# A state-space layer on one core: a new order of work inside a step on four engines

## The reference

```python
xn = layernorm(x)                                   # (2, 1024, 512)
proj = einsum('bld,pd->blp', xn, in_proj_w)         # gate 4096, x 4096, B 1024, C 1024, dt 64
xBC = silu(causal_conv(proj[x, B, C], taps=4) + conv_bias)
dt = softplus(dt + dt_bias); dA = exp(-dt * exp(A_log))
state = state * dA + (dt * x) (outer) B             # per head, 64 heads of 64, 128 states
y = state . C + x * D                               # scan over the tokens
yn = y * rsqrt(mean(y*y over a group of 512) + eps) * norm_weight * silu(gate)
s = einsum('bli,di->bld', yn, out_proj_w)
g = silu(xn @ W.T + bias + lora(xn))
out = x + s * g
```

## Time and profile before

| | |
|---|---|
| median of 3 runs | 1976.13 us (1975.52 to 1976.61) |
| the profiled execution | 1979.57 us, its span 1977.8 us |
| mean granted TensorE clock | 0.968 |
| busy: PE, DVE, POOL, ACT | 90%, 76%, 64%, 55% |
| steps 0 to 127: first and last output product | 137.5 us, 1970.2 us |

### The profile page before, as it was taken

How to read it: one execution, slowest core, us unless ns; L and a number is a source line. 1 busy time by engine, 2 the same in 40 slices (tenths; PEclk the granted TensorE clock), 3 DMA queues, 4 the chain that set the end, 5 groups by cost and what they waited for, 6 DMA issues and landing times.

```text
span 1977.8 us, 31470 instructions
## 1 busy us (share of the span) xinstructions
PE 1787.2 (90%) x10792; PEld 1373.7 (69%) x10792; DVE 1507.0 (76%) x1711; ACT 1087.7 (55%) x2843; POOL 1260.1 (64%) x1255
## 2 busy tenths in 40 slices
PE   7989989898998989899788998989899898989976
PEld 5767767676776767677566776767677676767754
DVE  8858778686877868687666877868687787868785
ACT  4566555655655565555445555565565556555543
POOL 6438475674847567484787847567484756748466
PEclk9999999999999999999899999999999999999988
DMA  7545445353544545355675554546354454635445
GB/s 254 156 139 171 142 136 170 120 181 105 167 145 138 169 121 181 108 172 162 181 232 156 170 147 139 168 122 181 106 169 144 136 165 125 181 107 155 146 135 162
DMA packets 322414, 304.75 MB, mean 154 GB/s; under 512 B 88272, under 2 KB 255568, under 8 KB 322256
## 3 DMA queue, kind: packets, MB, share of 16 engines
q1 hardware_dynamic: 321216, 302.60, 50.9%
q10 hardware_dynamic: 1040, 0.16, 0.0%
HBM read 246.57 MB, written 56.10 MB: 153 GB/s over the span
## 4 chain that ended last, share of the span: by engine, by line
POOL 42%; issue 31%; DVE 15%; ACT 9%; PE 2%; DMA 1%; SPq 0%; POOLq 0%; ACTq 0%; DVEq 0%
POOL cpre L1259 14%; POOL skip L1282 6%; POOL wconv_lo L1160 5%; POOL square L1305 4%; DVE ynt_lo L1140 4%; POOL wout_lo L1160 4%; POOL wgate_lo L1166 4%; ACT ps_y L807 4%; DVE xc L922 3%; DVE out_sum L1134 2%; POOL rstd_col L1313 2%; ACT stage L869 2%; DVE ps_y L1108 1%; POOL square_sum L1308 1%; POOL out_sum L1212 1%
## 5 line engine op out<-in xcount | busy, mean ns | idle before, releaser
L922 DVE SCALAR_TENSOR_TENSOR xc<-ps_conv,convw_sb,xc 128x511 f32<-128x511 f32 (+2 forms) x576 | 430.2, 747 | 149.9 <-ACT xc L693 136.4
L1305 POOL TENSOR_TENSOR square<-square 128x256 f32<-128x256 f32 x128 | 95.1, 743 | 442.9 <-ACT square L848 442.9
L1057 DVE TENSOR_TENSOR_SCAN decay<-decay,eye 128x1024 f32<-128x1024 f32 x125 | 362.9, 2903 | 0.0
L1259 POOL TENSOR_TENSOR cpre<-cpre,xc 128x1024 f32<-128x1024 f32 x112 | 300.4, 2682 | 0.0
L1350 PE MATMUL ps_out<-wout_hi,ynt_hi 128*128 128x512 f32 x512 | 161.6, 442 | 124.9 <-DVE out_sum L1134 105.6
L838 ACT ACTIVATE dtx<-x_tok,prefix_dt 128x64 f32<-128x64 f32 x1024 | 257.3, 336 | 6.5 <-DMA b_tok<-turned_d 6.5
L820 ACT ACTIVATE mean_square<-ps_g,eps 128x1 f32<-128x1 f32 x128 | 33.5, 261 | 409.9 <-PE ps_g L1343 409.9
L1509 PE MATMUL ps_y<-decay,dtx 128*64 128x128 f32 x1984 | 192.6, 281 | 32.5 <-DVE decay L1077 29.6
L1350 PE MATMUL ps_conv<-xn_hi,wconv_hi 128*128 128x512 f32 x768 | 217.7, 405 | 0.0
L1350 PEld LDWEIGHTS ps_out<-wout_hi,ynt_hi 128*128 128x128 f32 x512 | 98.4, 206 | 168.6 <-DVE out_sum L1134 129.3
L1134 DVE SCALAR_TENSOR_TENSOR out_sum<-ps_out,rstd_col,out_sum 128x512 f32<-128x512 f32 x108 | 80.5, 745 | 166.4 <-POOL rstd_col L1313 138.1
(11 more groups left out here) (233 smaller groups left out, 4105.6 us busy)
## 6 DMA issues: line engine op xcount, KB each, us to landing
decay<-decays_d SPq DMA_DIRECT2D x125, 512.0 KB, 5.0
cpre<-rows_d SPq DMA_DIRECT2D x112, 512.0 KB, 3.8
turned_d<-squares SPq DMA_DIRECT2D x512, 80.0 KB, 1.8
stage<-w_in_t SPq DMA_DIRECT2D x32, 1024.0 KB, 5.3
x_tok<-turned_d SPq DMA_DIRECT2D x128, 256.0 KB, 3.3
stage<-w_out_t SPq DMA_DIRECT2D x16, 1024.0 KB, 5.6
stage<-w_in_t SPq DMA_DIRECT2D x32, 256.0 KB, 3.2
b_tok<-turned_d SPq DMA_DIRECT2D x128, 64.0 KB, 3.6
```

The source lines that it names most:

```text
L922: e.scalar_tensor_tensor(acc[:, d:], ps[:, 0:BLK - d], convw_sb[:, tile, TAPS - 1 - d:TAPS - d], acc[:, d:], ALU.mult, ALU.add).then_inc(S ...
L1057: e.tensor_tensor_scan(d, d, eye8[:, :, :].rearrange("p h i -> p (h i)"), 0.0, ALU.mult, ALU.add).then_inc(scanned(i)[0], 1)
L1259: e.tensor_tensor(cpre[k % 2][:, :, :], cpre[k % 2][:, :, :], xc[i // CPB % 2][:, XT + 1, block_cols(i % NCH)].unsqueeze(1).to_broadcast([ ...
L1305: e.tensor_tensor(square[:, 0:2 * P], square[:, 0:2 * P], square[:, 2 * P:], ALU.add).then_inc(S["sum1"], 1)
```

## The change

In each step the instructions are the same; their order inside the step is another.

- **POOL** before: `skip`, splits of weights, `cpre`, both adds of squares, `rstd_col`, state decay, `xw`, edges. After: edges, `cpre`, `skip`, first add of squares, `rstd_col`, second add, state decay, `xw`, splits.
- **ACT** before: late convolution, `mean_square`, late SiLU, split of `wout`, `dtx`, `square`, early convolution, `ynt_hi`, gate SiLU, seed. After: late convolution, `dtx`, late SiLU, `square`, `mean_square`, `ynt_hi`, early convolution, seed, split of `wout`, gate SiLU. The halves of the gate's split and B and C's are at `at` = 3, 4 and 5 in place of 3, 5 and 4. From step 124 on the seed stays behind the gate SiLU.
- **DVE**: the scan is ahead of the late tile's taps, `last` stays behind them; the mixing matrix is ahead of the early tile's taps.
- **SP**: the tokens of the next step are fetched right after their store; the fetches of B and C's weights, of the x part's and of `wout` come one step later.

```diff
@@ sync
                 if i + 1 < N:
                     store_turned(i + 1)
+                    fetch_tokens(i + 1)
...
-                    if at == 3:
+                    if at == 4:
                         fetch_conv_bc(g + 1)
-                    if at == 5 and left > 1:
+                    if at == 6 and left > 1:
                         fetch_conv_x(g + 2)
-                    if at == 6:
+                    if at == 7:
                         fetch_out(g + 1)
-                if i + 1 < N:
-                    fetch_tokens(i + 1)
@@ scalar
                 if 0 <= m < N and conv_late(m) is not None:
                     conv(conv_late(m))
-                if u >= 0:
...
-                    e.activation(mean_square[:, u % 2:u % 2 + 1], ps_g[:, 2 * P:2 * P + 1], ACT.Identity, bias=eps[:, :],
-                                 scale=1.0 / GC).then_inc(S["var2"], 1)
-                if 0 <= m < N and conv_late(m) is not None:
-                    silu(conv_late(m))
-                if i < N and at == 1:
-                    w.wait_ge(S["scaled"], XT * (g + 1))
-                    w.wait_ge(S["mm_ffn"], KT + TOK)
-                    w.wait_ge(S["mm_out"], NCH * g)
-                    split_hi(wout_hi, staged(0, DM), range(XT), S["hi_out"])
                 if i < N:
...
                     scaled.then_inc(S["dtx"], 1)
+                if 0 <= m < N and conv_late(m) is not None:
+                    silu(conv_late(m))
                 if 0 <= m < N:
...
                     e.activation(square[:, :], y_bank(m)[:, :], ACT.Square).then_inc(S["square"], 1)
-                if i < N and conv_early(i) is not None:
-                    conv(conv_early(i))
+                if u >= 0:
+                    w.wait_ge(S["mm_ssq"], u + 1)
+                    w.wait_ge(S["rstd2"], u - 1)
+                    w.wait_ge(S["half"], 2)
+                    e.activation(mean_square[:, u % 2:u % 2 + 1], ps_g[:, 2 * P:2 * P + 1], ACT.Identity, bias=eps[:, :],
+                                 scale=1.0 / GC).then_inc(S["var2"], 1)
                 if 0 <= m < N:
...
                     e.activation(ynt_hi[:, :, :], turns(y_bank(m)), ACT.Copy).then_inc(S["hi2"], 1)
+                if i < N and conv_early(i) is not None:
+                    conv(conv_early(i))
+                if i < TAIL:
+                    seed(i)
+                if i < N and at == 1:
+                    w.wait_ge(S["scaled"], XT * (g + 1))
+                    w.wait_ge(S["mm_ffn"], KT + TOK)
+                    w.wait_ge(S["mm_out"], NCH * g)
+                    split_hi(wout_hi, staged(0, DM), range(XT), S["hi_out"])
                 for k in gated(i):
                     gate_silu(k)
+                if TAIL <= i < N:
+                    seed(i)
                 if i < N:
-                    seed(i)
                     if at == 3 and left:
                         split_gate(g + 1, (0, 1))
-                    if at == 5 and left:
+                    if at == 4 and left:
                         split_gate(g + 1, (2, 3))
...
-                    if at == 4 and left:
+                    if at == 5 and left:
                         split_conv_bc(g + 1, range(KT))
@@ vector
-                if 0 <= m < N and conv_late(m) is not None:
-                    taps(conv_late(m))
...
                     if i <= TAIL:
                         scan(i)
+                if 0 <= m < N and conv_late(m) is not None:
+                    taps(conv_late(m))
+                if i < N:
+                    if i <= TAIL:
+                        last_factors(i)
                     if i + 1 < N:
                         turn(i + 1)
...
+                if i <= TAIL:
+                    mixing_matrix(i)
                 if i < N and conv_early(i) is not None:
                     taps(conv_early(i))
-                if i <= TAIL:
-                    mixing_matrix(i)
@@ gpsimd
+                if i < N and i % NCH == 0:
+                    edges(group(i))
+                if i < N and i % NCH > 0:
+                    left_of_state(i)
                 if i < N:
...
                                     ALU.mult).then_inc(S["skip"], 1)
+                if 0 <= m < N:
+                    bm, cm, gm = batch(m), m % NCH, group(m) % GROUPS
+                    w.wait_ge(S["square"], m + 1)
+                    e.tensor_tensor(square[:, 0:2 * P], square[:, 0:2 * P], square[:, 2 * P:], ALU.add).then_inc(S["sum1"], 1)
+                if u >= 0:
+                    col = slice(u % 2, u % 2 + 1)
+                    w.wait_ge(S["var2"], u + 1)
+                    w.wait_ge(S["osum"], u - 1)
+                    e.tensor_tensor(rstd_col[:, col], mean_square[:, col], half[:, :], ALU.pow).then_inc(S["rstd2"], 1)
+                if 0 <= m < N:
+                    w.wait_ge(S["sum1"], m + 1)
+                    w.wait_ge(S["mm_ssq"], m)
+                    e.tensor_tensor(square_sum[:, :], square[:, 0:P], square[:, P:2 * P], ALU.add).then_inc(S["sum2"], 1)
+                    if cm < NCH - 2:
...
+                        e.tensor_tensor(by_head(dec[:, :]), by_head(new[:, :]), heads_bc(total_bc[:, first:first + GH]),
+                                        ALU.mult).then_inc(S["sdec"], 1)
+                if i < N and i % NCH < NCH - 1:
+                    scale_x(i)
                 if i < N:
                     g, at = divmod(i, NCH)
                     left = BATCH * GROUPS - 1 - g
...
-                if i < N and i % NCH > 0:
-                    left_of_state(i)
-                if 0 <= m < N:
...
-                if i < N and i % NCH < NCH - 1:
-                    scale_x(i)
-                if i < N and i % NCH == 0:
-                    edges(group(i))
```

More of the change, by code:

```diff
@@ L1058, in scan, with last_factors @@
                                      ALU.mult, ALU.add).then_inc(scanned(i)[0], 1)
+            def last_factors(i):
+                d = decay_room(i)
                 if i % NCH < NCH - 1:
@@ L1136, in _ @@
                     scan(AHEAD[i - TAIL + 3])
+                    last_factors(AHEAD[i - TAIL + 3])
                 if 0 <= m < N:
```

39 lines of the change are left out of this document (11 added, 28 removed).

## The result

| | before | after |
|---|---|---|
| median | 1975.83 us (1973.04 to 1976.61, 4 runs) | 1855.88 us (1850.06 to 1857.94, 4 runs) |
| profiled execution, its span | 1979.57, 1977.8 us | 1856.4, 1854.3 us |
| mean granted TensorE clock | 0.968 | 0.984 |

The ratio is 0.9391 (95% interval 0.9367 to 0.9414): 6.1% faster, 120 us.

A forecast was written before the change was run, and what follows sets the result against it. PE was taken as the bound, losing time to waits down a POOL-DVE-PE chain. Fourteen groups at 7.6 (106.4), 2.4 for the first and 13.6 for the finishing one gave 122.4 us: 1857.2 profiled, 1854 median, range 1790 to 1930.

The forecast's parts named there:

- What bounds the kernel: PE, busy 90% of the span, is the engine to fill; an eight-step group takes 115.2 us, 104.1 without losses.
- POOL as the source of the long wait: PE's 5.48 us wait for `out_sum` in the wout step, explained by POOL's splits (5.77 us) ahead of `rstd_col`.
- ACT: `square` sooner: On ACT, `dtx` moves into the wait for late taps and `square` directly follows `y`: some 2.7 us earlier.
- Mixing matrix: On DVE, ahead of the early taps, done 2.3 us earlier, more than PE's waits of 0.98 and 0.89 us.
- The split of `wout` becomes late: ACT's and POOL's later `wout` split stalls PE's third pass 0.1 to 2.4 us; 2.4 taken per group.
- Half of the clock's loss comes back: Of 2.37 us a group lost to PE's lower clock behind the long wait, half counted as still lost, 1.2.
- Contention at nothing: POOL and DVE sharing memory: nothing beyond the medians taken; the other bound was 2.0 us each for scan and `last` per step.
- the scan's median staying at 2.3 us: Sign on DVE that the forecast holds; a median scan near 4 would show it wrong.
- the slower rival: DVE becomes the bound through collisions of scan and `last`, loop 16.9 us, 2101 us in all; chance 0.12.
- SP priced at nothing: Tokens' fetch ahead of the weights' and three weight fetches a step later: covered, some 5 us of cover left for `wout`.
- The finishing groups: Group finishing the first sequence gains 7.6 + 6.0 = 13.6 us as splits fill POOL's wait; the last counted as ordinary.
- the group of 107.6: Sign on PE: a group of eight steps takes near 107.6 us.

The follow-up runs named there:

- w_early: Changed kernel with ACT's split of `wout` right behind `ynt_hi` and POOL's right behind its second add of squares: 1803.6 us.
- a_only: Kernel before with only ACT's order new (`dtx`, late SiLU, `square` ahead of `mean_square`), its split of `wout` still ahead of `dtx`: 1897.3 us.
- u_split: Changed kernel with POOL's whole order, ACT's `wout` split, its halves' steps and SP's weight fetch steps put back as before: 1836.1 us.
- u_mix: Changed kernel with DVE's mixing matrix put back behind the early tile's taps: 1864.0 us.
- w_pool: Changed kernel with only POOL's split of `wout` moved earlier, right behind the second add of squares: 1856.6 us.
- f_front: Changed kernel with SP's store of a finished output and the loads for the next ahead of the tokens' store and fetch: 1843.6 us.
- wf: Changed kernel with the edits of `w_early` and `f_front` together: 1797.9 us.
- s_back: Changed kernel with SP's order as before, the tokens' fetch behind the weights' and three weight fetches one step earlier: 2051.3 us.
- am: Kernel before with ACT's order of `a_only` plus DVE's mixing matrix ahead of the early taps: 1921.0 us.

## Why the prediction was right, and where it was not

The time (1854, measured 1855.9) and the direction were right. Step by step:

- **What bounds the kernel**: right. PE was the engine to fill; with the waits gone it is busy 102.90 of 102.90 us in `w_early`, and the group is 1.2 us shorter than the 104.1 of the working.
- **POOL as the source of the long wait**: wrong in its attribution. The waits for `out_sum` did go, as the prediction has it. But "POOL has the time, but in the wrong place" read the 5.77 us of splits between ACT's high parts and `rstd_col` as POOL's delay. The 5.96 us in front of them were ACT's. It is ACT's queue (`mean_square`, late SiLU, `dtx` ahead of `square`) that `a_only` shortens, with POOL untouched, and there the long wait falls from 5.5 to 1.9 us; in `u_split` it is gone with the splits still in front of `rstd_col`. POOL's order alone makes the kernel 121 us slower. Together with the other orders it need not be a loss: `w_early`, which keeps most of it, is 32 us faster than `u_split`, which does not.
- **ACT: `square` sooner**: right in direction, too small in rank. The prediction names 2.7 us and gives it no term of its own; alone it is worth 80 us, more than any other part that was run alone.
- **Mixing matrix**: right. The term was 0.98 + 0.89 a group, 28 us over 15 groups; alone it measured 25. In the full change its move is worth only 8, and not in front of `y`: with ACT's and SP's orders it is hardly late even behind the taps (1.8 us in all in `u_mix`). Nor does it add to ACT's order: on top of `a_only` it costs 24.
- **The split of `wout` becomes late**: right, and the best of the steps. Forecast 2.4 us in front of the third pass at POOL's low parts; measured 2.45, 39.3 us over 16 waits, with the scan among the splits as forecast. Its source was ACT's place in the order (`w_early` against `w_pool`), which the step's count from `ynt_lo` over the seed contains. It was left out for group 0, which has this wait too and so lost 0.5 us where 2.4 of gain was forecast.
- **Half of the clock's loss comes back**: too low. In ten groups all of it came back, the other 1.2 us; this, with some 0.7 of shorter matmuls where no wait stands in front of them any more, is the 1.9 by which they beat the forecast.
- **Contention at nothing** (but for the scan among the splits of `wout`): near enough as a price, wrong as a fact. The forecast sign "the scan's median staying at 2.3 us" failed. The lengths of the changed kernel (ns, minimum/median/maximum):

```profile
L1059 DVE TENSOR_TENSOR_SCAN decay<-decay,eye x125: 2247/2689/4415, 111.0 to 1792.7; 128x1024 f32<-128x1024 f32 x125
...
L1070 DVE TENSOR_TENSOR last<-decay,prefix_dt x110: 164/200/2009, 113.3 to 1795.0; 128x16 f32<-128x16 f32 x110
```

  The scan's median rose from 2284 to 2689. Counted in the two timelines, 77 of all 132 scans run beside a split of weights (33 before), and 19 beside no instruction of POOL (47 before). The loop over DVE stayed under PE's step all the same: DVE is busy 80% of the span, and the steps without a wait take PE's 14.49 and 11.77 us. The two-input rule of the Trainium skill (GPSIMD Engine Reference, "Key points") fits these rows as it fitted those of before, the taps' mean being 745 ns here; it does not say which of two orders collides less, and the slower rival that was priced from it did not come.
- **SP priced at nothing**: wrong, though it left no mark on the sum, which is luck. The edit was looked at for what it delays (the weights) and found covered; what it prevents was not asked. Without it the changed kernel takes 2051 us: the slower rival's size, by another mechanism than the one named for it.
- **The finishing groups**: the terms were mis-sized. Group 7 gained 17.6 in place of 13.6, but groups 8 and 15, counted as ordinary, lost 1.8 and 0.1 where 7.6 each was forecast. Part of the cause is in SP's order: with `f_front` groups 7, 8 and 15 are 3.5, 3.4 and 4.3 us shorter, and of the 17.1 missed in 8 and 15 together that is 7.7. Another part of group 8 can be read in the changed kernel's timeline: PE waits there 4.26 us for `out_sum` (at 991.40) and 4.11 for ACT's high parts of `wout` (at 1011.03), of which 3.46 and 0.52 are left in `w_early`. What holds group 8 at 113 to 115 us even in `w_early` and `wf` stays open.

So the direction and the rough size came from a right reading of where PE waits. That the sum came within 1 us of the measured gain is luck: some 23 us of terms that were too low and as many that were too high cancelled. And the runs turned round the attribution of the main gain. Of the forecast signs, those on waits were met (POOL's wait for `square` fell from 442.9 to 258.8 us), the group of 107.6 only in groups 1 and 2, and the scan's median not at all.

## What to carry to other kernels

An order written by hand is one thing across all queues: of four reordered engines here, one alone gave 80 us, a part of one 25, one cost 121 alone and would have cost 195 in the whole without the fourth's edit, which looks free; and two that gain alone, 80 and 25, gave 56 together. So for each instruction moved later, ask what it frees and which in-order queue stands behind that (here: split, staging slot, weight fetch, tokens, `dtx`, `square`). And what PE waits for at the end of a chain is not where the time is lost: follow it up to the first engine that was late, and test the parts alone, before the gain is put down to the part that stands next to the wait.

## What the runs showed of the hardware

**A wait does not always cost the clock.** In the changed kernel PE waits some 2.5 us at the same place in each ordinary group; its matmuls stay at the upper level behind it in ten of twelve (the next first pass takes 1.07 us, as above), and the clock falls in groups 1 and 2. The first of those, and a longer wait in group 7:

```profile
253.32 0.97 PE L1367 MATMUL ps_out<-wout_lo,ynt_hi 128*128 128x512 f32 x3 [2.84 <-POOL wout_lo L1171]
...
255.74 0.64 PE L1520 MATMUL ps_y<-decay,dtx 128*64 128x128 f32 x4
...
933.05 2.08 PE L1361 MATMUL ps_out<-wout_hi,ynt_hi 128*128 128x512 f32 x4 [5.49 <-DVE out_sum L1143]
```

Behind 2.84 us the product of `y` takes 0.64 in place of 0.44; behind 5.49 us the first pass takes 2.08 in place of 1.07, as behind the 5.46 and 5.48 of the earlier trace rows. The length of the wait alone does not decide: in `s_back` a wait of 2.45 us at the same place was followed by a granted clock of 0.91 over the step (group 4), in the changed kernel by 1.00 (group 11). Two short waits can be better than one long one: 1.20 and 1.82 us in `a_only` left the clock at 1.00, the 3.31 us of `am` at the same place brought it to 0.79 in the step behind.

**A wait costs more than itself.** At the upper level, too, the matmuls behind it take longer: the first pass of the output product 1.15 to 1.21 us behind waits of 0.33 to 1.20, in place of 1.07.

**POOL and DVE lengthen each other by up to a whole instruction.** POOL's add of 256 columns took 2.71 us beside the scan in `am` (mean 0.74 over the kernel before), the scan 4.29 beside `cpre` (2.25 at the shortest), and the four splits of `wout` 6.99 in the changed kernel against 5.77.
